# Input surveys and batch 0's quantised branch moved from the opening into steps 0 to 8

## The reference

```python
xn = _layernorm(x, axis=-1)
s = _L0_attn_ref(xn, Wq, bq, Wk, bk, Wv, bv, Wo, bo, sinks)
g = _silu(_L0_ffn_ref(xn, weight, weight_scale, bias))
x = x + s * g
# attention: 32 query heads, 8 key/value heads of width 64, rotary turn of queries and keys,
# scores kept where |row - column| <= 128, a sink logit per head in the softmax, projection Wo
# ffn: scale = max(max|xn| / 448, 1e-7) over all batches; x_q = float8_e4m3(xn / scale);
#      x_q @ (weight * weight_scale).T + bias
```

## Time and profile before

| | us |
|---|---|
| median of 3 runs | 1682.67 |
| the three runs | 1677.29, 1682.67, 1683.79 |
| the profiled execution, its own time | 1678.36 |
| its span in the trace | 1676.5 |
| TensorE busy | 1621.8 |
| VectorE busy | 1143.2 |
| GpSimd busy | 1037.8 |

### The profile page before, as it was taken

How to read it: one execution, slowest core, us unless ns; L and a number is a source line. 1 busy time by engine, 2 the same in 40 slices (tenths; PEclk the granted TensorE clock), 3 DMA queues, 4 the chain that set the end, 5 groups by cost and what they waited for, 6 DMA issues and landing times.

```text
span 1676.5 us, 34111 instructions
## 1 busy us (share of the span) xinstructions
PE 1621.8 (97%) x11183; PEld 1457.1 (87%) x11183; DVE 1143.2 (68%) x3619; ACT 989.7 (59%) x2407; POOL 1037.8 (62%) x1016
## 2 busy tenths in 40 slices
PE   6599999999999999999999999999999999999998
PEld 4388988989898988989889898898988899898987
DVE  7756676767676667667677667676676667666664
ACT  2456665566655665656655666556655566556663
POOL 5656665676666657576576656567566666656651
PEclk9799999999999999999999999999999999999999
DMA  6644534544544543534554443643544544443550
GB/s 200 137 86 95 107 66 91 95 79 92 86 86 89 92 89 70 116 65 88 93 84 94 89 91 67 113 85 73 106 72 87 100 78 98 80 86 70 95 99 13
DMA packets 77278, 150.89 MB, mean 90 GB/s; under 512 B 12720, under 2 KB 25264, under 8 KB 73008
## 3 DMA queue, kind: packets, MB, share of 16 engines
q1 hardware_dynamic: 77104, 148.71, 45.9%
HBM read 18.64 MB, written 4.19 MB: 14 GB/s over the span
## 4 chain that ended last, share of the span: by engine, by line
PE 90%; DVE 3%; ACT 3%; issue 2%; DMA 1%; POOL 1%; SPq 0%; POOLq 0%; DVEq 0%
PE pv_bank L1283 29%; PE ring L1176 13%; PE ring L1241 11%; PE acc L1308 10%; PE score L1267 8%; PE score L1269 8%; PE ring L1293 4%; PE ring L1185 2%; PE ring L1166 1%; PE ring L1213 1%; ACT qT_high L711 1%; ACT prob_all L676 1%; PE acc L1192 1%; DMA gate<-in_w_all 1%; DVE junk L989 1%
## 5 line engine op out<-in xcount | busy, mean ns | idle before, releaser
L989 DVE CUSTOM_DVE_ANT_0 junk<-ring,mask,sink 128x384 bf16<-128x384 f32 (+1 forms) x1024 | 558.4, 549 | 291.8 <-PE ring L1241 273.2
L1283 PEld LDWEIGHTS pv_bank<-v,prob_all 128*128 128x128 f32 x5120 | 682.3, 191 | 30.7 <-ACT prob_all L676 11.5
L1283 PE MATMUL pv_bank<-v,prob_all 128*128 128x65 f32 x5120 | 685.4, 265 | 3.5 <-DVE o_norm L1004 1.3
L580 POOL TENSOR_SCALAR_AFFINE_SELECT prob_all<-prob_all 128x512 f32<-128x512 f32 x384 | 254.5, 677 | 450.2 <-ACT prob_all L676 450.1
L676 ACT ACTIVATE prob_all<-score 128x512 f32<-128x512 f32 x640 | 370.2, 595 | 172.8 <-PE score L1269 161.9
L1241 PE MATMUL ring<-kT_high,qT_full 128*128 128x384 f32 (+1 forms) x1024 | 371.7, 363 | 16.6 <-DVE row_max L989 7.9
L1267 PE MATMUL score<-qT_full,kT_high 128*128 128x512 f32 x640 | 263.9, 412 | 0.7
L1269 PE MATMUL score<-qT_high,kT_low 68*128 68x512 f32 x640 | 254.8, 398 | 0.0
L1241 PEld LDWEIGHTS ring<-kT_high,qT_full 128*128 128x128 f32 x1024 | 196.1, 191 | 50.4 <-DVE row_max L989 20.0
L734 ACT ACTIVATE oT_hi<-ring 128x256 fp32r<-128x256 f32 x256 | 96.5, 377 | 182.1 <-PE ring L1293 180.9
L1010 DVE TENSOR_TENSOR oT_lo<-ring,oT_hi 128x256 fp32r<-128x256 f32 x256 | 107.8, 421 | 135.9 <-ACT oT_hi L734 134.1
(11 more groups left out here) (137 smaller groups left out, 2582.0 us busy)
## 6 DMA issues: line engine op xcount, KB each, us to landing
qT_high<-qT_full SPq DMA_DIRECT2D x64, 512.0 KB, 4.5
qT_full<-q_first SPq DMA_DIRECT2D x64, 256.0 KB, 4.2
qT_full<-q_first_hi SPq DMA_DIRECT2D x64, 256.0 KB, 5.5
qT_full<-q_second SPq DMA_DIRECT2D x64, 256.0 KB, 4.2
qT_full<-q_second_hi SPq DMA_DIRECT2D x64, 256.0 KB, 5.4
kT_high<-k_first_hi SPq DMA_DIRECT2D x128, 64.0 KB, 2.5
kT_high<-k_second_hi SPq DMA_DIRECT2D x128, 64.0 KB, 2.5
x_res<-in_x SPq DMA_DIRECT2D x10, 512.0 KB, 6.2
```

Source lines behind the costliest of these rows:

```text
L580: nc.gpsimd.affine_select(out=pr, in_=pr, compare_op=ALU.is_ge, fill=0.0, base=0, pattern=[[0, GROUP], [sign, P]], channel_multiplier=-sign) \
L989: nc.vector.tensor_tensor_reduce(junk[:, h % 2, 0:cols], ring[h % 2][:, 0:cols], mask[:, m0:m0 + cols], 1.0, sink[:, col:col + 1], ALU.add ...
L1283: last = nc.tensor.matmul(pv[:, h, :], prob[:, q % 2 * 3 + n, h * P:(h + 1) * P], v[:, slot, k, :], start=(n == 0), stop=(n == len(BLOCKS[ ...
```

## The change

Three surveys stay in the opening (1, 2, 3); 4 and 5 go to step 0, 6 to step 1, 7 to step 2, each cut into `survey_spread`, `survey_max` and `survey_min` that stand in different quarters. The largest value of batch 0's own rows goes to step 1, `widest` to the end of step 2, `largest` and its two matmuls to step 3. Batch 0's quantising goes to steps 3 and 4, its turned copy to step 4, `ffn` to steps 5 and 6, the gate to steps 5 to 8, in a new buffer x_late; the next batch's statistics to step 4 and its normalisation to step 5. VectorE rotates the first queries straight from PSUM (`first_queries_turn`) and GpSimd only adds them up (`first_sums`). GpSimd, not VectorE, makes the remainders of chunks 2 and 3, and the later chunks come in another order (`CHUNK_ORDER`) and later. SP loads chunks 2 and 3 ahead of the constants. TensorE projects keys, first queries and three value tiles in a row into banks of their own; in place of 32 + 12 idle matmuls it makes 14 small ones (`warm`), 16 and one behind each row matmul of step -1. Some small buffers share their place with others (ident, ones, var_eps, x_var). The diff, cut to its core and shifted to the left:

```diff
-FIRST_CHUNKS = 2 * KT
+CHUNK_ORDER = (0, 1, 2, 3, 6, 4, 7, 5, 8, 9, 10)
...
+def high_count(n):
+    return CHUNK_ORDER.index(n) + 1
+def low_count(n):
+    return CHUNK_ORDER.index(n) - KT + 1
...
+    if n == 0 and (k, q) in ((4, 1), (4, 2)):
+        return ("xq", 0, q - 1)
     if (k, q) == (0, 2):
-        return ("xq", n, 1) if 0 <= n < BATCH else None
+        return ("xq", n, 1) if 1 <= n < BATCH else None
...
+def ffn_at(n, k, q):
+    slots = ((5, 0), (6, 0)) if n == 0 else ((1, 0), (1, 2))
+    return slots.index((k, q)) if 0 <= n < BATCH and (k, q) in slots else None
...
+        x_late = sb("x_late", [P, TILES, M], F32)
+        ffn_e_first = x_late[:, 0:2, :]
...
+        turns = [(k_bias[:, :], b_k), (cos[:, :], rope_cos), (sin[:, :], rope_sin), (q_bias[:, :], b_q)]
+        consts = [(v_bias[:, :], b_v.partition_broadcast(P)), (sink[:, :], sinks.partition_broadcast(P)),
...
+    [buf[:, :, :].rearrange("p t m -> p (t m)") for buf in (gate, x_res, ffn_e, x_late)]
+        chunk_at_first = (0, 1, 2, 3, 6, 6, 2, 5, 6, 4, 6)
+        x_at_first = (4, 0, 1, 3, 4, 3, 4)
...
+        if it == 0:
+            sp.wait_ge(s_late_lo_done, low_count(4))
+            load_chunk(5)
+            sp.wait_ge(s_row_done, 4)
+            load_first_x(6)
+        if it == 1:
+            sp.wait_ge(s_row_done, 5)
+            load_first_x(7)
+        if it == 4:
+            sp.wait_ge(s_xq_done, 2)
+            sp.dma_start(x_in[:, :, :], x_t[1]).then_inc(s_x_got, 16)
...
         if it == 0:
-            sp.wait_ge(s_xq_done, 2)
-            sp.dma_start(x_in[:, :, :], x_t[1]).then_inc(s_x_got, 16)
-        if it == -1:
-            sp.wait_ge(s_row_done, 6)
-            load_chunk(FFN_CHUNK + 1)
-        if it in (0, 2):
-            sp.wait_ge(s_late_lo_done, FFN_CHUNK + 2 + it // 2 - FIRST_CHUNKS)
-            load_chunk(FFN_CHUNK + 2 + it // 2)
-        if k == 4 and 0 <= n < BATCH:
+            sp.wait_ge(s_late_lo_done, low_count(5))
+            load_chunk(8)
+        if it == 1:
+            sp.wait_ge(s_row_done, 7)
+            load_chunk(9)
+            sp.wait_ge(s_late_lo_done, low_count(8))
+            load_chunk(10)
+        if it == 6 or k == 4 and 1 <= n < BATCH:
...
+    load_chunk(2)
+    load_chunk(3)
+    for dst, src in turns:
+        sp.dma_start(dst, src).then_inc(s_turn_in, 16)
+    load_first_x(1)
     for dst, src in consts:
         sp.dma_start(dst, src).then_inc(s_const_in, 16)
-    load_chunk(2)
-    load_chunk(3)
-    load_first_x(1)
+    sp.wait_ge(s_w_lo_done, 1)
+    load_first_x(2)
+    load_chunk(4)
+    sp.wait_ge(s_late_lo_done, low_count(2))
+    load_chunk(6)
+    sp.wait_ge(s_w_lo_done, 2)
+    load_first_x(3)
     load_chunk(FFN_CHUNK)
-    for m in range(2, 6):
-        sp.wait_ge(s_w_lo_done, m - 1)
-        load_first_x(m)
+    sp.wait_ge(s_late_lo_done, low_count(3))
+    load_first_x(4)
     keys_high_in(0)
-    sp.wait_ge(s_row_done, 1)
-    load_first_x(6)
     queries_in(0, False)
     queries_in(0, True)
-    sp.wait_ge(s_row_done, 2)
-    load_first_x(7)
     keys_low_in(0)
-    sp.wait_ge(s_row_done, 3)
-    load_chunk(4)
-    sp.wait_ge(s_row_done, 4)
-    load_chunk(5)
-    sp.wait_ge(s_row_done, 5)
-    load_chunk(W_CHUNKS)
+    sp.wait_ge(s_row_done, 1)
+    load_first_x(5)
...
+    def first_sums():
+        pool.wait_ge(s_rope, 3)
+        nc.gpsimd.tensor_tensor(q_first[:, :], q_first[:, :], q_second_hi[:, :], ALU.subtract) \
+            .then_inc(s_rope, 1)
+        pool.wait_ge(s_rope, 5)
         nc.gpsimd.tensor_tensor(q_second[:, :], q_second[:, :], q_odd[:, :], ALU.add).then_inc(s_rope, 1)
...
+            if it == 0 and q == 0:
+                chunk_low(4)
+            if it == 2 and q == 3:
+                rows_rstd(5, 7)
...
-            if it in (0, 1, 3) and q == (0 if it == 0 else 3):
-                chunk_low(FFN_CHUNK + 1 + (it + 1) // 2)
+            if it == 0 and q == 0:
+                chunk_low(FFN_CHUNK)
+            if it == 0 and q == 3:
+                chunk_low(5)
+            if it == 1 and q == 0:
+                rows_rstd(1, 4)
+            if it == 1 and q == 3:
+                chunk_low(8)
+            if it == 3 and q == 0:
+                chunk_low(9)
+            if it == 3 and q == 3:
+                chunk_low(10)
     rstd_of(0)
+    chunk_low(2)
+    chunk_low(3)
     keys_sum(0)
-    turn_even(0)
-    turn_odd(0)
-    turn_rest(0)
+    first_sums()
     first_low(0)
     second_low(0)
     keys_low(0)
-    rows_rstd(1, 4)
+    chunk_low(6)
     turn_even(1)
     turn_odd(1)
     turn_rest(1)
     first_low(1)
     second_low(1)
-    chunk_low(4)
-    rows_rstd(5, 7)
-    for n in range(5, FFN_CHUNK + 1):
-        chunk_low(n)
...
+                act.wait_ge(s_late_lo_done, low_count(6))
+                act.wait_ge(s_row_done, 3)
...
-            if it == -1:
-                chunk_high(FIRST_CHUNKS + q)
-            if it in (0, 1, 3) and q == (0 if it == 0 else 1):
-                chunk_high(FFN_CHUNK + 1 + (it + 1) // 2)
-            if (k, q) in ((2, 2), (4, 2)) and 0 <= n < BATCH:
+            if it == -1 and q == 0:
+                chunk_high(6)
+                chunk_high(4)
+                chunk_high(FFN_CHUNK)
+            if it == 0 and q == 3:
+                chunk_high(5)
+            if it == 1 and q == 2:
+                chunk_high(8)
+            if it == 2 and q == 3:
+                chunk_high(9)
+            if it == 3 and q == 2:
+                chunk_high(10)
+            if it == 3 and q == 1:
+                scale_x(0)
+            if it in (5, 6) and q == (1 if it == 5 else 3):
+                ffn_exp(0, it - 5)
+            if (k, q) in ((2, 2), (4, 2)) and 1 <= n < BATCH:
...
     chunk_high(1)
+    chunk_high(2)
     for k in range(KT):
         x_high(0, k)
-    chunk_high(2)
     chunk_high(3)
-    even_out(0)
     keys_first_high(0)
     keys_second_high(0)
-    odd_out(0)
...
-    def survey(m):
+    def survey_spread(m):
         buf, i = first_x(m), (m - 1) * TILES
         dve.wait_ge(first_x_in[m - 1], 16)
...
         for t in range(TILES):
             nc.vector.bn_stats(stats[:, t, :], buf[:, t, :]).then_inc(s_row_bn, 1)
-        nc.vector.tensor_reduce(x_ends[:, i:i + TILES], buf, AX.X, ALU.max)
-        nc.vector.tensor_reduce(x_ends[:, ROWS + i:ROWS + i + TILES], buf, AX.X, ALU.min) \
-            .then_inc(s_row_done, 1)
         for t in range(TILES):
...
-    def widest():
+    def survey_max(m):
+        i = (m - 1) * TILES
+        nc.vector.tensor_reduce(x_ends[:, i:i + TILES], first_x(m), AX.X, ALU.max)
+    def survey_min(m):
+        i = ROWS + (m - 1) * TILES
+        nc.vector.tensor_reduce(x_ends[:, i:i + TILES], first_x(m), AX.X, ALU.min).then_inc(s_row_done, 1)
+    def widest_first():
         nc.vector.tensor_reduce(x_ends[:, 2 * ROWS:], x_in[:, :, :], AX.XY, ALU.max,
                                 apply_absolute_value=True).then_inc(s_row_self, 1)
+    def widest():
...
+    def first_queries_turn(odd):
+        dve.wait_ge(s_q_pe, odd + 1)
+        parts = ((q_second_hi, sin), (q_odd, cos)) if odd else ((q_first, cos), (q_second, sin))
+        for dst, turn in parts:
+            nc.vector.scalar_tensor_tensor(dst[:, :], score[odd][:, :], q_bias[:, odd:odd + 1], turn[:, :],
+                                           ALU.add, ALU.mult).then_inc(s_rope, 1)
     def values(m, t):
...
-        bank = score[t - 1] if m == 0 and t in (1, 2) else ring[1]
+        bank = (pv_bank, acc[0], ring[2], ring[1])[t] if m == 0 else ring[1]
...
-            if q == 1:
-                survey(7)
-            elif q == 3:
-                widest()
+            return
+        if n == 0:
+            if it == 0:
+                if q == 0:
+                    survey_spread(4)
+                    survey_max(4)
+                elif q == 1:
+                    survey_min(4)
+                elif q == 2:
+                    survey_spread(5)
+                else:
+                    survey_max(5)
+                    survey_min(5)
+            elif it == 1:
+                if q == 0:
+                    survey_spread(6)
+                elif q == 1:
+                    survey_max(6)
+                    survey_min(6)
+                elif q == 3:
+                    widest_first()
+            elif it == 2:
+                if q == 0:
+                    survey_spread(7)
+                elif q == 1:
+                    survey_max(7)
+                    survey_min(7)
+                elif q == 3:
+                    widest()
+            elif (k, q) == (3, 0):
                 largest()
-            return
-        if (k, q) in ((0, 0), (0, 1)) and n == 0:
-            if q == 0:
-                dve.wait_ge(s_late_lo_done, FFN_CHUNK + 1 - FIRST_CHUNKS)
-            exponents(0, q)
-            quantise(0, q)
-            quantised(0, q)
+            elif (k, q) == (3, 2):
+                dve.wait_ge(s_late_lo_done, low_count(FFN_CHUNK))
```

(84 more changed lines are left out.)

146 lines of the change are left out of this document (72 added, 74 removed).

## The result

The changed kernel takes 1670.81 us, the median of six runs (1669.61 to 1672.12), against 1683.23 of the kernel before (1677.29 to 1686.17): a ratio of 0.9933 [0.9918, 0.9948], 12.4 us less. That is faster by more than 0.5% and inside the range of 1649 to 1673, but 10.8 us above the 1660 forecast. Measured once more with the last set of experiments, the same kernel came out at 0.9948 [0.9930, 0.9967].

A forecast was written before the change was run, and what follows sets the result against it. VectorE was taken to bound the opening, TensorE the 64 steps. Opening gain 20.3 plus old waits 11.5 minus new waits 11.9 gave 19.9 us, so 1658.5 from the profiled execution, set to 1660; range 1649 to 1673.

The forecast's parts named there:

- the two regimes: Whole kernel: an opening that VectorE sets, then 64 steps that TensorE sets.
- the prediction's own sign: Prediction counts as wrong if the opening or the distance from step 0 to step 8 is off by over 10 us.
- step 5's excess of 2.0 us: Step 5: four normalisations and a clamp, 2.5 us plus one meeting with GpSimd, stall TensorE by 2.0 us.
- Slower: Rival: quarters exceeding the room make TensorE stand 2.8 us, then run at lower clock, 4.3 us each; chance 0.05.
- Step 6's 1.2 us: Step 6: the wait of the kernel before stays, 1.2 us.
- the 1.8 us of room: Each quarter step: up to 1.8 us of added VectorE work costs nothing, covered by TensorE's queue.
- The late end of 15.5 us: Opening: keys start at 15.5 us if GpSimd's remainder goes first on the shared port; 14.4 was kept.
- the transfer costs 0 to 0.5 us: Opening: the first queries' transfer, needed by 37.3 us, lands at 35 to 37.9, costing 0 to 0.5 us.
- the 8.2 us from there to step 0: End of the opening: eight wide row maxima 6.1 us and four narrow 2.1, so step 0 starts at 45.5 us.
- Steps 1 and 2, the surveys and the largest value: Added VectorE work: excess 0.5 us each in steps 1 and 2, 0.8 for the largest value's two products.
- Step 3's quantising and the late queries: Step 3: scale chain 0.5 us, quantising beside GpSimd 1.3 + 1.0, queries' last transfer 1.5 us late.
- Moved waits come back: Rival: port meetings and late second queries raise the excess to 16 to 19 us; 1664 to 1672 us, chance 0.14.

The follow-up runs named there:

- e1_norm_q0: Changed kernel with batch 1's four normalisations on VectorE moved from quarter 1 to quarter 0 of step 5; 1665.20 us, ratio 0.9896.
- e13_invert_early: Changed kernel with the last reciprocal of the feed-forward's first half moved from quarter 2 to quarter 0 of step 6; 1670.05 us, ratio 0.9925.
- e12_norm_early: Changed kernel with batch 1's normalisations in quarter 0 of step 5 and GpSimd's earlier start on the second queries; 1660.08 us, ratio 0.9872.
- e9_early_turn_alone: Changed kernel with only an earlier start of GpSimd's second queries; 1667.51 us, ratio 0.9915.
- e10_small_first: Changed kernel whose three opening surveys read only 16 of each row's 256 columns; 1673.24 us, ratio 0.9946.
- e11_gpsimd_rotates: Changed kernel with the first queries again copied out by ScalarE and rotated by GpSimd instead of VectorE; 1677.36 us, ratio 0.9969.
- e3_small_surveys: Changed kernel whose four surveys in steps 0 to 2 read only 16 of each row's 256 columns; 1670.04 us, ratio 0.9922.
- r_before: The kernel before, unchanged, measured once more for a second profile; 1685.94 us.

## Why the prediction was wrong

The sign held, and so did the two regimes; the size did not. By the prediction's own sign, neither part is off by more than 10 us (3.0 and 9.4 below), but both miss to the same side. The account is made against the profiled executions, as the forecast was: 1678.36 us before and 1671.91 after, 6.5 us less where 19.9 was forecast. Of the 13.4 us that are missing, 3.0 lie in the opening, 9.4 in steps 0 to 7 (an excess of 217.9 - 196.6 = 21.3 us, forecast 11.9) and about 1 behind them.

**The step that failed: step 5's excess of 2.0 us.** In e1_norm_q0 step 5's TensorE work at full clock is 26.6 us; the changed kernel's 34.3 us are 7.7 over it, so 5.7 of the 9.4 lie there. I priced four normalisations and a clamp at "2.5 us plus one meeting". Shown by e1_norm_q0: the place of the normalisations alone costs 7.05 us, 2.2 of them idle TensorE and the rest the lower clock behind it, and with it gone only 0.6 us of idle time is left. Two errors made it. The forecast asked where GpSimd works only for step 3, and gave step 5 one meeting; in quarter 1 GpSimd begins the queries of every step, and three of four short instructions each took as long as one of its operations: 4.34 us together instead of 1.70. The Trainium skill, page "SBUF — State Buffer", section "Who interferes with whom", names tensor_scalar, which has one such input, among the operations that can take the pair of ports which VectorE shares with GpSimd, where its operands allow it, and says that the one which comes first keeps it for a whole instruction. The trace agrees on the length: a median of 1376 ns beside operations of 1.3 us, 406 ns without; on who comes first it does not always, as the opening shows. And the forecast's own price of a quarter that exceeds the room, 2.8 us of standing and then the lower level, stood in the rival *Slower* and not in this term.

**Step 6's 1.2 us** was taken over from the kernel before, and as idle time it held, although the change puts a reciprocal of 0.95 us ahead of the exponents there: 0.83 and 0.32 us after the change, and in the kernel before, in its timeline of TensorE:

```profile
243.07 0.28 PE L1213 MATMUL ring<-ident_r,neg_parts 128*4 128x128 f32 x2 [0.76 <-DVE oT_lo L1010]
243.90 0.85 PE L1283 MATMUL pv_bank<-v,prob_all 128*128 128x65 f32 x6 [0.32 <-DVE o_norm L1004]
```

There the exponents alone took 1.54 and 1.39 us beside GpSimd, and here the quarter has 0.95 + 0.73 + 1.40: both are over the 1.8 us of room. What the sum lacked is the lower clock behind these waits, which comes in some executions only: step 6 takes 29.95 or 27.05 us after the change and 28.99 or 25.90 before. The forecast rested on a profile without it and is compared here with one that has it, so 2.9 us of the miss depend on which executions were profiled; the 1.1 us by which the step is longer either way are TensorE work that moved there (25.82 us busy in e1_norm_q0, 24.75 before). e13_invert_early shows that without the reciprocal there the waits go.

**The opening, 3.0 us short.** The keys started at 12.93, sooner than 14.4 and than the early bound: VectorE's two remainders took 1.2 us each, as long as before the change without GpSimd beside them, and GpSimd's took 3.51 us instead of 2.36. So the meeting went against GpSimd, which was not on the path. In the changed kernel's timeline of VectorE and GpSimd:

```profile
9.33 2.35 DVE L940 TENSOR_TENSOR w_lo<-prob_all,w_hi 128x1024 fp32r<-128x1024 f32 x2
...
10.39 3.51 POOL L543 TENSOR_TENSOR w_lo<-prob_all,w_hi 128x1024 fp32r<-128x1024 f32 x1 [2.40 <-ACT w_hi L691]
...
13.87 2.36 POOL L543 TENSOR_TENSOR w_lo<-gate,w_hi 128x1024 fp32r<-128x1024 f32 x1
```

The late end of 15.5 us did not come although its condition did: chunk 2's high part was ready by 10.39, before VectorE's first remainder ended (half of 2.35 us from 9.33). In e12_norm_early GpSimd's remainder is recorded from 10.00, before VectorE's second (two of 1.2 us from 9.47), and still ended only at 14.04, its 2.4 us after VectorE's second. Which engine waits, then, is not decided by the earlier recorded start alone; these traces do not show the rule.

Key turn at 15.99 (forecast near 17), query turns end at 23.0 (23.3), first row matmul at 37.01 (by 38): right, and so was "the transfer costs 0 to 0.5 us". The failed term is the 8.2 us from there to step 0, 6.1 + 2.1 for twelve maxima with nothing for a wait: measured 11.50, from 37.01 to 48.51, of which 2.04 are the wait for the negated maxima and 1.3 slower maxima. Where it comes from: GpSimd may write its query buffers only when the first queries have landed, so its eight operations start at 37.08, and ScalarE's rounding of the second half, which needs six of them, starts only at 44.78. The negated maxima stand behind that rounding in ScalarE's order:

```profile
44.78 0.63 ACT L745 ACTIVATE q_second_hi<-q_second 128x512 fp32r<-128x512 f32 x1 [1.95 <-POOL q_second L565]
```

The lower clock of step 0's first ten wide matmuls follows. The forecast followed this chain only to the second landing, for which it allowed 0 to 2 us; that landing (56.39, not 51 to 53) holds up nothing in the changed kernel, but ScalarE's order in between does. e9_early_turn_alone, e10_small_first and e11_gpsimd_rotates show from three sides that this chain, not VectorE, ends the opening.

**What held.** Steps 1 and 2, the surveys and the largest value: e3_small_surveys puts them near 1.5 us, the forecast had 3.4 with their consequences. Step 3's quantising and the late queries, 4.3 us in the forecast, cost less than that: steps 2 and 3 took 49.2 us, 2.4 more than before, surveys included. Step 4, for which nothing was forecast, holds the x turns moved there and waits of 0.88 and 1.03 us.

**The base.** The forecast went 1.5 us above its own execution. r_before shows an execution 7.6 us slower by lower clock in steps 0 and 6, and most runs lie nearer to it. Measured against that one, steps 0 to 7 became only 1.1 us longer (216.8 and 217.9 us). This fits medians that differ by 12.4 us where the two profiles differ by 6.5.

**The rivals.** What came is nearest to *Moved waits come back*: the excess of 21.3 us lies beyond its 16 to 19, and both of its causes were at work, the port meetings and the late second queries (through ScalarE's order, not their landing), though two quarters were enough for it. That the time lies in its span of 1664 to 1672 says less: its gain of 13 to 16 us gives 1664 to 1667 by the prediction's own base, and the median of 1670.81 is in the span only because its upper end was set wider. A kernel of the size that was forecast exists once the two losses are out: e12_norm_early takes 1660.08 us, its opening 21.8 us sooner (forecast 20.3) and its excess 13.8 us (11.9).

Left open: why the same wait is followed by 20 us at the lower level in one execution and by none in another, which also decides 3 us of step 6, and the 1 us behind step 8.

## What to carry to other kernels

Before moving short VectorE instructions, lay GpSimd's timeline beside the quarter that they go to: a quarter with one busy GpSimd operation after another prices each at up to that operation's length, while the same step's first quarter, 8 us away, left TensorE no wait above 0.49 us. When the work that led a stretch is taken out, follow the next chain through the buffers it reuses, not only through the engines; here it was landing, GpSimd, ScalarE's order. And take the sum's base from two profiled executions if their clocks differ: a wait that cost 1.1 us in one cost about 3 more in the other.

## What the runs showed of the hardware

A tensor_scalar of 128x256 took 0.41 us alone and up to 1.42 beside GpSimd's products, and GpSimd's remainder of 128x1024 took 3.51 us (4.04 in e12_norm_early) instead of 2.36 beside VectorE's: either engine can be the one that waits. A 2.45 us wait of TensorE was followed by a granted clock of 0.50 for 20 us in one execution and by 1.00 in another of the same kernel. Waits of 0.83 and 0.32 us were followed by a granted clock of 0.50 (236 to 240 us in the changed kernel) and waits of 0.87 and 0.33 us in e1_norm_q0 by 1.00. The four query transfers of 256 KB, issued within 2.6 us in the opening, landed 8.4 to 9.1 us after the last issue in the changed kernel and every variant of it, with and without a 512 KB load beside them; in a middle step, with the first two 4 us ahead, 5.4 us.
